# Two atom pursuits run half an image apart, with marked Gram rows, gathered Gram cells and the reconstruction added in memory

## What is computed

```python
x = x + conv3x3_circular(gn(x), weight)          # 64 -> 64 channels
x = x + sparse_code(gn(x), dictionary)           # patches of 64*4*4 = 1024 values, 512 atoms

def sparse_code(z, dictionary):                  # orthogonal matching pursuit, K_MAX = 5
    D = dictionary / (norm(dictionary, axis=0) + 1e-10)
    G = D.T @ D + 1e-5 * eye(512)
    h_bar = (D.T @ X).T ; h = h_bar              # X: one column of 1024 values for each patch
    for k in 1..5:
        index = argmax(abs(h * ~mask)); mask[index] = True     # an atom is taken once
        L, x_stack = Cholesky row and solve with G[I, index]   # I: the atoms so far
        h = h_bar - x_stack @ G[I]
    return D @ coefficients                      # 1024 patches an image
```

## Time and profile before

| | |
|---|---|
| median of 3 runs | 4907.73 us |
| span of the profiled execution, first to last instruction | 4899.8 us |
| PE busy | 3743.9 us (76%) |
| DVE busy | 4216.4 us (86%) |
| ACT busy | 2323.6 us (47%) |
| POOL busy | 1584.6 us (32%) |
| mean granted TensorE clock | 0.891 |
| DMA queues of SP and POOL, share of 16 engines | 9.0% and 9.2% |

### The profile page before, as it was taken

The page is one execution under the profiler, slowest core; times in us unless marked ns, Lnnn a source line. Parts: engine busy times, 40 slices in busy tenths (PEclk is TensorE's granted clock), DMA queues, the critical chain, the costliest instruction groups (busy, mean ns, idle before and its releaser), DMA issues. The chain is left out here.

```text
span 4899.8 us, 49570 instructions
## 1 busy us (share of the span) xinstructions
PE 3743.9 (76%) x9968; PEld 1762.2 (36%) x9968; DVE 4216.4 (86%) x10489; ACT 2323.6 (47%) x4435; POOL 1584.6 (32%) x1221
## 2 busy tenths in 40 slices
PE   7877887878788787887877788787877877778724
PEld 3333333433333333333433333343333433333312
DVE  2399898888989889898898989889898888989997
ACT  5673545536354463545536354462535536355210
POOL 0133323333323333323333323333323333323342
PEclk8988998989899998998999899998988989899867
DMA  3001222112120301222121120301222121120211
GB/s 100 18 26 65 65 70 61 30 64 62 63 70 26 99 28 61 65 70 62 31 72 53 64 70 26 100 28 59 66 70 61 31 73 53 63 70 28 66 32 47
DMA packets 189483, 277.75 MB, mean 57 GB/s; under 512 B 12112, under 2 KB 147536, under 8 KB 180816
## 3 DMA queue, kind: packets, MB, share of 16 engines
q0 software_dynamic: 40960, 134.25, 9.2%
q1 hardware_dynamic: 148176, 139.90, 9.0%
HBM read 205.95 MB, written 68.16 MB: 56 GB/s over the span
## 5 line engine op out<-in xcount | busy, mean ns | idle before, releaser
L860 PE MATMUL conv_ps<-xn,wc 128*128 128x512 f32 x3072 | 1424.9, 625 | 245.7 <-ACT xn L508 186.5
L442 POOL DMA_INDIRECT u<-gram_rows,idx x512 | 533.5, 1042 | 2084.0 <-DVE idx L636 1954.3
L841 PE MATMUL gen_ps<-dn,z 128*128 128x512 f32 x2048 | 952.9, 626 | 311.4 <-ACT z L479 267.0
L430 POOL TENSOR_TENSOR h<-h,mask 128x512 f32<-128x512 f32 x512 | 801.4, 1587 | 1129.8 <-DVE h L767 1129.8
L823 PE MATMUL gen_ps<-ct,dt 128*128 128x512 f32 x2048 | 983.6, 638 | 127.3 <-DVE xa L566 115.0
L534 ACT ACTIVATE score<-h 128x512 f32<-128x512 f32 x640 | 372.1, 593 | 1338.9 <-POOL h L430 1093.1
L860 PEld LDWEIGHTS conv_ps<-xn,wc 128*128 128x128 f32 x3072 | 608.3, 200 | 1039.6 <-issue 885.0
L657 DVE CUSTOM_DVE_ANT_0 junk<-u,hot 128x512 bf16<-128x512 f32 x1088 | 719.8, 704 | 0.0
L841 PEld LDWEIGHTS gen_ps<-dn,z 128*128 128x128 f32 x2048 | 407.4, 201 | 853.7 <-issue 531.2
L823 PEld LDWEIGHTS gen_ps<-ct,dt 128*128 128x128 f32 x2048 | 408.1, 204 | 679.3 <-issue 486.6
L759 DVE SCALAR_TENSOR_TENSOR u<-u,nl 128x512 f32<-128x512 f32 x768 | 589.9, 828 | 12.8 <-DVE na L702 2.1
(11 more groups left out here) (79 smaller groups left out, 2601.1 us busy)
## 6 DMA issues: line engine op xcount, KB each, us to landing
xa<-x_pairs SPq DMA_DIRECT2D x64, 1024.0 KB, 6.1
y_pairs<-xa SPq DMA_DIRECT2D x64, 1024.0 KB, 6.1
u<-gram_rows,idx POOLq DMA_INDIRECT x512, 3.5
dn<-atoms SPq DMA_DIRECT2D x1, 2048.0 KB, 7.7
xa<-x_pairs SPq DMA_DIRECT2D x32, 64.0 KB, 6.0
gram_rows<-u SPq DMA_DIRECT2D x4, 256.0 KB, 2.0
wc<-w_taps SPq DMA_DIRECT2D x6, 48.0 KB, 6.0
ident<-ident_in SPq DMA_DIRECT2D x1, 64.0 KB, 7.4
```

Of the source, the lines that this page charges most:

```text
L430: pool.tensor_tensor(h[:, g * T + t, :], h[:, g * T + t, :], mask[:, t, :], ALU.mult)\
L442: pool.indirect_dma_start(u[:, t, k, :], None, gram, bass.IndirectOffsetOnAxis(ap=idx8[:, t, 0:1], axis=0))\
L841: last = pe.matmul(gen_ps[t % 2][:], z[:, t % 2, d // PATCH, d % PATCH, :], dn[:, d, :], start=(d == 0), stop=(d == ND - 1))
L860: last = pe.matmul(conv_ps[c % 2][:], wc[:, m, :], xn[:, c % XN_RING, rows:rows + CP, tap:tap + W], start=(m == 0), stop=(m == 2 * TAPS - 1))
```

## The change

**Groups half an image apart.** A period is now 10 units of 4 slots, listed in `UNITS` as (lag, group, k): group 0 works on image i-1, group 1 runs half an image later and takes the last two steps of image i-2. A unit is algebra and projection of step k-1 and then the search of step k, and the units of the two groups alternate, so that a gather is issued one unit of the other group before its rows are used. All pursuit semaphores and the rows `u` are doubled or shared by `ROW_OF`. The plans are written anew (`lag` now 2 for co, ce, ct, re), PE's sequence is written anew, with the convolution cut into pieces between turns, reconstructions and correlations. The coefficient rows have a ring of 4 places.

**Marked diagonal.** A second copy of the Gram matrix in memory has 1e16 added on its diagonal. After an update with such a row, h is huge at the places taken, so no mask is multiplied; the search skips values over 1e5.

**Sign by search.** FIND_INDEX8 now looks in h itself (with 8 more columns, in SBUF) for +best and -best; the smaller index is the atom and the comparison gives the sign, so h is not picked.

**Gram cells by gather.** The k earlier cells G[I, index] of a tile are fetched from memory, each by an indirect DMA of its own of 128 single values, and not picked from rows; since these are cells of G and not of projected rows, the Cholesky row needs a forward substitution (2(k-1) small instructions).

**Reconstruction added in memory.** SP stores the convolved image when its residual addition is done; ACT copies each reconstruction step from PSUM to a buffer `rb` (1 MB, one buffer), and POOL adds it to the output in memory by an accumulating DMA, 4 an image. The output array has the layout (image, group, phase, partition, 16, 128).

**Other.** The descriptor scratch of the dynamic DMAs is 8192, 4 periods are unrolled ahead of the loop and 4 behind it, and the last periods now run to images + 1.

```diff
+UNITS = ((1, 0, 0), (2, 1, 3), (1, 0, 1), (2, 1, 4), (1, 0, 2), (1, 1, 0), (1, 0, 3), (1, 1, 1), (1, 0, 4), (1, 1, 2))
+VECTOR_PLAN = {
+    0: [("gn", 0, 1), ("co", 0), ("gn", 0, 2), ("ce", 0, 0), ("ce", 0, 1)],
+    2: [("ca", 0), ("ce", 0, 2)], 2.5: [("ce", 0, 3)], 3.5: [("ca", 1)],
+    7.5: [("ca", 2)], 8.5: [("ca", 3)], 9.5: [("ca", 4)], 12.5: [("ca", 5)], 13.5: [("ca", 6)],
+    19: [("ca", 7)], 19.5: [("ca", 8)], 20: [("co", 1), ("ce", 1, 0), ("ca", 9), ("ce", 1, 1)],
+    22: [("ce", 1, 2), ("ca", 10)], 22.5: [("ce", 1, 3)], 23.5: [("ca", 11)],
+    24.5: [("ca", 12)], 25.5: [("ca", 13)], 28.5: [("ca", 14)], 29.5: [("ca", 15)],
+    31.5: [("gn", 1, 1)], 32: [("gn", 1, 2)],
+}
+SCALAR_PLAN = {
+    0: [("rt", 0), ("xn", 0), ("ct", 0, 0)], 1: [("ct", 0, 1), ("xn", 1)],
+    3: [("ct", 0, 2), ("xn", 2), ("ct", 0, 3), ("xn", 3)], 5: [("xn", 4)],
+    7: [("re", 0, 0), ("re", 0, 1), ("re", 0, 2), ("re", 0, 3), ("xn", 5), ("z", 4), ("xn", 6)],
+    11: [("re", 0, 4), ("re", 0, 5), ("re", 0, 6), ("re", 0, 7), ("xn", 7), ("st", 9), ("xn", 8), ("z", 5)],
+    13: [("xn", 9)], 15: [("h", 4), ("xn", 10), ("z", 6), ("h", 5), ("z", 7)], 17: [("h", 6)],
+    19: [("h", 7), ("xn", 11), ("st", 10), ("st", 11)], 20: [("ct", 1, 0)], 21: [("ct", 1, 1), ("xn", 12)],
+    23: [("ct", 1, 2), ("xn", 13), ("ct", 1, 3), ("st", 12), ("xn", 14), ("st", 13), ("st", 14)],
+    27: [("xn", 15), ("st", 15), ("re", 1, 0), ("re", 1, 1), ("re", 1, 2), ("re", 1, 3)],
+    31: [("re", 1, 4), ("re", 1, 5), ("st", 16), ("st", 17), ("re", 1, 6), ("re", 1, 7), ("rt", 1), ("z", 0), ("z", 1)],
+    34: [("z", 2)], 35: [("h", 0), ("h", 1), ("z", 3), ("st", 0), ("st", 1), ("st", 2)],
+    37: [("h", 2), ("st", 3), ("st", 4)], 39: [("h", 3), ("st", 5), ("st", 6), ("st", 7), ("st", 8)],
+}
+ADD_PLAN = {1: (0, 0), 2: (0, 1), 6: (1, 0), 7: (1, 1)}
...
-                            pool.tensor_tensor(h[:, g * T + t, :], h[:, g * T + t, :], mask[:, t, :], ALU.mult)\
-                                .then_inc(h_masked, 1)
...
+            def gather(img, g, k):
+                if k > 0:
+                    stop_until(cell_found[g], at(img, KMAX - 1, k))
+                    for t in range(T):
+                        for j in range(k):
+                            pool.indirect_dma_start(
+                                v[:, g, k, j, t:t + 1], None, cells,
+                                bass.IndirectOffsetOnAxis(ap=cell[:, g, k // (KMAX - 1), j, t:t + 1], axis=0))\
+                                .then_inc(v_loaded[g] if k < KMAX - 1 else v_last[g], 16)
+                if k < KMAX - 1:
+                    stop_until(atom_found[g], at(img, KMAX - 1, k + 1))
+                    for t in range(T):
+                        pool.indirect_dma_start(u[:, t, ROW_OF[g][k], :], None, marked,
+                                                bass.IndirectOffsetOnAxis(ap=chosen[:, g, t:t + 1], axis=0))\
+                            .then_inc(row_loaded[g][t], 16)
+            def add(img, g, ph):
+                stop_until(recon_out, at(img, GROUPS * ND, g * ND + (ph + 1) * PATCH))
+                stop_until(x1_out[g * PHASES + ph], at(img, 16, 16))
+                pool.dma_start(out[number(img)][g, ph], rb[:], accum_op=ALU.add).then_inc(recon_added, 16)
             def period(i, par, loop=False):
+                for n, (back, g, k) in enumerate(UNITS):
+                    if here[back]:
+                        gather(apart(i - back, g), g, k)
+                    if here[2] and n in ADD_PLAN:
+                        add(i - 2, *ADD_PLAN[n])
...
+                elif kind == "re":
+                    act.wait_ge(recon_done, at(img, GROUPS * ND, g * ND + d + 1))
+                    if pj == 0 and not (isinstance(img, int) and img == 0 and g == 0 and ph == 0):
+                        act.wait_ge(recon_added, at(img, 16 * GROUPS * PHASES, 16 * (g * PHASES + ph)))
+                    act.activation(rb[:].rearrange("p h (w j) -> p j h w", j=PATCH)[:, pj],
+                                   gen_ps[d % 2][:].rearrange("p (h w) -> p h w", h=HR), ACT.Copy).then_inc(recon_out, 1)
...
-                dve.wait_ge(recon_done, at(img, GROUPS * ND, g * ND + d + 1))
-                dve.tensor_tensor(dst, gen_ps[d % 2][:].rearrange("p (h w) -> p h w", h=half // 2), dst, ALU.add)\
...
+            def search(img, g, k, between):
+                for t in range(T):
+                    stop_until(score_ready[g], at(img, STEPS, k * T + t + 1))
+                    dve.max(top8[:, t, :], score[t % 2][:]).then_inc(top_found[g], 1)
+                between(2)
...
+                between(2.5)
+                for t in range(T):
+                    dve.max_index(idx8[:, t, :], h[:, g * T + t, ATOMS:HW], h[:, g * T + t, :]).then_inc(located[g], 1)
+                between(3)
...
+                between(3.5)
             def factor_row(g, k, wait, step, n, tmp_, squares, total, pivot):
+                for j in range(k - 1):
+                    dve.tensor_tensor(tmp_[:, j + 1:k, :], nl[:, g, j + 1:k, j, :], ...)
+                    dve.tensor_tensor(v[:, g, k, j + 1:k, :], v[:, g, k, j + 1:k, :], tmp_[:, j + 1:k, :], ALU.add)
...
             def period(i, par, loop=False):        # tensor engine, all parts present
+                average(i, 0)
+                turn(i - 2, 0, (0, 1)); convolve(i, range(0, 1)); turn(i - 2, 0, (2, 3)); convolve(i, range(1, 2))
+                recon(i, 0, 0, here); convolve(i, range(2, 5)); recon(i, 0, 1, here); convolve(i, range(5, 7))
+                correlate(i, i - 1, range(T, TILES), here); convolve(i, range(7, 10))
+                turn(i - 2, 1, (0, 1)); convolve(i, range(10, 11)); turn(i - 2, 1, (2, 3)); convolve(i, range(11, 14))
+                recon(i, 1, 0, here); convolve(i, range(14, 16)); recon(i, 1, 1, here)
+                average(i, 1); correlate(i, i, range(T), here)
```

More of the change, by code:

```diff
@@ L140, in __add__, with apart @@
         return Image(self.turn, self.n + more)
+def apart(image, g):
+    return Image(image.turn + 1, image.n - 2) if g and not isinstance(image, int) else image
 def number(image):
@@ L405, in _ @@
+            periods(sp, period)
+            for n in range(GROUPS * PHASES):
+                sp.wait_ge(x1_out[n], 16 * images)
+            sp.wait_ge(recon_added, 16 * GROUPS * PHASES * images)
         @block.gpsimd
@@ L796, in _, with turn @@
         def _(pe):
-            def turn(img, g):
-                for t in range(T):
+            def turn(img, g, tiles):
+                for t in tiles:
                     n = g * T + t
@@ L850, in average, with convolve @@
                 pe.matmul(st_ps[:, 1:2], avg[:], gsc[:, 2:3], start=True, stop=True).then_inc(gn_sum, 1)
-            def convolve(i, between):
-                for c in range(CHUNKS):
+            def convolve(i, chunks):
+                for c in chunks:
                     pe.wait_ge(xn_ready, at(i, CHUNKS, c + 1))
@@ L877, in period @@
-                if b:
-                    recon(i - 1, 0, lambda done: average(i, 1) if own and done == AVERAGE_AFTER else None)
-                elif own:
+                if p:
+                    turn(i - 2, 0, (0, 1))
+                if own:
+                    convolve(i, range(0, 1))
+                if p:
+                    turn(i - 2, 0, (2, 3))
+                if own:
+                    convolve(i, range(1, 2))
+                if p:
+                    recon(i, 0, 0, here)
+                if own:
+                    convolve(i, range(2, 5))
@@ L905, in setup @@
     ones = h[:, 7, 0:P]
+    rows = [h[:, n, 0:ATOMS] for n in range(7)]
     with nc.Block() as block:
```

582 lines of the change are left out of this document (268 added, 314 removed), and 19 rows, old and new, of tables (SCALAR_PLAN, VECTOR_PLAN).

## The result

The changed kernel takes 5054.1 us (median of 4 runs, 5044.1 to 5055.8) against 4909.7 (4906.8 to 4912.9) of the kernel before, run beside it: ratio 1.0291, interval 1.0277 to 1.0306. It is **slower by 144 us**. The prediction said 4639 us, between 4290 and 4950, and gave 0.17 to slower.

What follows compares the result with a forecast made beforehand. DVE was taken to bound the kernel before; afterwards a walk through the engines' waits gave 276 us a period. 775 us for the ends + 14 x 276 = 4639 us, range 4290 to 4950.

Steps and rivals of the forecast that it cites:

- What bounds the kernel: DVE, 256.3 of 290 us a period, sets the time; the change takes it to about 170, no longer the bound.
- The gather's spacing: On POOL, time from one cell gather to the next: 1.25 us taken, bounds 0.98 and 1.53; 140 us a period.
- The addition: POOL's accumulating 1 MB DMA of a reconstruction: 6.1 us to landing, as a store, and 1 us for issuing.
- the walk: Following which engine waits for which through one period: 276 us a period, 4639 us in all; chance 0.43.
- The half rate: Case of the addition costing double, 12.2 us since two sources are read: period 288, 4807 us; chance 0.17.
- last part: After the final periods, group 1's steps 3 and 4, coefficients, turns and two reconstruction phases: about 160 us.
- the walk's 6 and 6: PE's waits for ACT's copies before the third reconstruction step, group 0 and group 1: 6 us each.
- its 3: PE's wait before the fifth reconstruction step of group 0, whose copy needs `rb` free after the addition: 3 us.
- step 1: Turn of the period: ACT's closing sums, average, factors, 21 `co` instructions at 0.2 bring first `ce` at 17.7; PE idles 18 us.
- steps 2, 5 and 7: Turns and chunks to 45; group 1's turns, chunks, phase to 218 with 6 us wait; last tiles and h copy to 277.
- the gather queue as the bound: Rival on POOL: a cell gather costs 2.2 us, not 1.25; period 306, 5059 us, slower; chance 0.17.
- PE-bound: Rival: waits of steps 3 to 6 are hidden by their neighbours; period 252, 4303 us; chance 0.2.

Runs made afterwards that it cites:

- straight line: The changed kernel with its ten looped periods written out, no loop: 4750.1 us on chip A, 5054.7 us on chip C.
- Early statistics and order: Changed kernel, next image's statistics spread over earlier scores (alone 4769.9 us, chip A), plus convolution chunks before transposes: both 5094.8 us, chip B.
- with the pause: Changed kernel with two small GpSimd memsets (0.65 us) after each tile's gathers of a step, chip E: 4965.7 us; with early statistics and order 4960.0.
- control on chip D: The changed kernel unedited, run beside the fourth set's edits: 5030.4 us, ratio 1.026.

## Why the prediction was wrong

*What bounds the kernel.* Right. DVE came to 167 us an image (170 predicted). It is 53% busy and not 60 to 65, since the period is longer, and PE 75% and not above 80. One premise doesn't fit the rows, though nothing was worked out from it: of the 683 us that DVE idled before, put 464 down to waits for PE's results and ACT's scores.

*The gather's spacing,* which I took as the widest unknown, was 1.25 us (chip C, at 720.00 and 721.24), the value taken. The sum wasn't wrong there.

*The addition.* I took a store's landing, 6.1 us. The list of DMA issues on chip A (count, size, us to landing) has a store and an addition side by side:

```profile
y_rows<-xa SPq DMA_DIRECT2D x64, 1024.0 KB, 7.4
y_rows<-rb POOLq DMA_DIRECT2D x64, 1024.0 KB, 8.4
```

So the term was 2.3 us too small, 2 x 2.3 = 4.6 us a period by the walk. Its weight there isn't confirmed: without additions the period on chip A is 275.7 (loop kept), and 281.7 with them (in the straight line), so all they cost is 6.0, where the walk has 4 to 5 with a landing of 6.1 and would have 9 to 10 with 8.4. The store beside it takes 7.4, so an addition costs 1.14 stores. The half rate that the Trainium skill gives a ReduceScatter against an AllGather in "Collectives: The Full Stack", Part 3 (the bandwidth ceiling), because the add reads two sources, isn't seen in this landing time; the measurement decides.

*The walk.* On chip A, where nothing is delayed, it comes within 2.5% (spans, us; the prediction's 8 outside the span left out):

| part | walk | straight line, A | changed kernel |
|---|---|---|---|
| to the second image's average | 217.4 | 220.9 | 220.7 |
| first period after it | 185 | 185.3 | 199.6 |
| thirteen periods | 13 x 276.0 = 3588 | 13 x 281.7 = 3662 | 13 x 300.5 = 3907 |
| from there to the end | 640.6 | 677.5 | 726.6 |
| span | 4631 | 4746 | 5054 |

Of the 115 us between the walk and chip A, 74 lie in the periods, 5.7 in each. The average comes 13.8 us after the tile and not 10.4; the rest, with smaller gains against it, wasn't taken apart. 37 lie in the end, which I didn't take apart either; the terms that the prediction lists for its last part (79, 17 and 50) add up to 146 and not to the 160 that it took, so the sum there was wrong as well. PE's waits stand nearly as walked, in this period of chip A with 6.46 and 5.67 for the walk's 6 and 6 (and 3.45 for its 3, not shown):

```profile
2096.23 0.59 PE L788 MATMUL st_ps<-mv,avg 128*128 128x1 f32 x2 [13.78 <-ACT mv L305]
2104.22 4.36 PE L741 MATMUL ct_ps<-ident,ce 128*128 128x128 f32 x20 [6.12 <-DVE ce L533]
...
2142.52 8.76 PE L764 MATMUL gen_ps<-ct,dt 128*128 128x512 f32 x16 [6.46 <-ACT rb L425]
...
2290.28 9.96 PE L764 MATMUL gen_ps<-ct,dt 128*128 128x512 f32 x16 [5.67 <-ACT rb L425]
```

*The step that failed* is step 1, and with it every place where I wrote "21 small instructions of `co` at 0.2" and closing sums at "about 2": **the price of a small dependent instruction** was read from a trace in which POOL issues 32 gathers a period. With 112, in runs of up to 28, it is 0.7 to 1.4 us in some stretches, in every set of runs with the unedited kernel in it, and these stretches lie on the path at the turn of the period and ahead of the transposes. The same term, the time from the end of one instruction to the start of what waits for it, stands at nothing in steps 2, 5 and 7, where DVE and ACT wait for PE's transposes, chunks and correlated tiles: there the increments come up to 6.2 us late, and in the straight line on chip C that is 291 of the 428 us of idle time behind late increments, against 131 in DVE's own chains. On chip A the sum is 0. The two runs are 305 us apart.

*The rivals.* The one called slower, the gather queue as the bound, gave 5059 us and a period of 306, close to what came, but by another mechanism: that it came near is luck. Its price, 2.2 us a gather, was wrong, and DVE waits 74 us in the whole run for gathers. What was right in it is that the cell gathers are the cause. PE-bound was refused by the same waits as in the walk: 6.46, 3.45 and 5.67 us on chip A.

*Early statistics and order,* which theory S had as the cure, gave next to nothing: on chip A TensorE's wait for the average fell from 13.8 to 2.1 us, but the period became 284.0 and not shorter than the straight line's 281.7, since DVE then waited 3.8 us for the fifth step's cells ahead of `co`, and the transposes 10.3 us for `ce`. The idle time moved along the chain. S wasn't tested on more than that one kernel on chip A; on chip E, with the pause, early statistics and order together gave 6 us (4966 and 4960).

*Open:* why the chips differ, and whether it is the chips at all: each was used in one set only, so the chip can't be told from what else was different at that time; what holds the increments up on their way; from which rate or length on. Another order of the gathers, and the additions ahead of a block, weren't tried, and the unedited kernel wasn't run on chips A and E.

## What to carry to other kernels

A price read from a trace holds for the load under which it was read. Where a change multiplies the number of DMAs, also ask what they do to the semaphores that everybody else waits on, and look for chained small steps whose gaps grow and for "remote" among the releasers. Run the unedited kernel in every set of experiments: without it four edits looked like four cures, when they had fallen on the one chip that showed no delays.

## What the runs showed of the hardware

- Indirect gathers of 128 values each 1.25 us, in unbroken runs of 12 to 28, go with late semaphore increments of PE, ACT and DVE in four of the six sets of measurements (not on chip A; on chip E only kernels with a pause ran). In DVE's chains a start 0.04 us after the end of the instruction before becomes 0.5 to 0.8 or 1.1 to 1.4 us (25 and 28 of the 62 in the control on chip D); an increment of PE comes up to 6.2 us late (chip C). It lasts 4 to 5 us past the start of the last gather. The same program takes 5055 us with it and 4750 without. Without the cell gathers, or with a pause of 2.6 us after each tile's, it is gone or nearly so. Every gather here raises its semaphore by 16, so a period has 112 x 16 = 1792 such increments instead of 32 x 16 = 512. The Trainium skill, "DMA: Bandwidth & Descriptors", "Why a DMA increments its semaphore by 16 and not by 1", says that in a DMA issued by GpSimd all 16 engines post their increment whatever its shape; the count here agrees (28619 increments recorded for the 1792 gathers of the straight line on chip A, 16 each), but that these increments are what crowds the others out was only argued, not shown.
- In the looped kernels many register and semaphore instructions of ACT's and DVE's sequencers took some 0.7 us in the delayed stretches (124 of 0.5 to 0.9 us on ACT in the unedited kernel on chip B); the straight line has hardly any such instruction to delay, and was no faster (5055 against 5042 us on chip C).
- The kernel before, with 32 gathers a period, was within 0.2% on all five chips (4902 to 4908 us), so a comparison with it doesn't tell on which kind of chip one is.
